# The 32 batches of a layer kernel written out without a loop, with every wait on a constant

## The reference, cut to what matters

```python
# attention: 16 heads of 16, causal and linear
q, k, v = relu(q), relu(k), v            # from xn @ wqkv
kv  = cumsum(k[..., :, None] * v[..., None, :], axis=tokens)
num = einsum('bhnd,bhnde->bhne', q, kv)
den = einsum('bhnd,bhnd->bhn', q, cumsum(k, axis=tokens)) + EPS
attention = (num / den) @ wo
# ffn: sigmoid router, top 2 of 8 experts, 4 of them are MLPs
hid = silu(xn @ Wg) * (xn @ Wu);  mlp_out = hid @ Wd
ffn = sum of cw * (mlp_out, xn, xn, relu(xn)) + causal depthwise conv(xn, 4 taps)
```

## Time and profile before

| | us |
|---|---|
| median of 3 runs | 1405.55 (1403.64 to 1406.98) |
| the profiled execution, its own time | 1406.35 |
| span of its trace | 1404.5 |
| PE busy | 1366.1 (97%) |
| DVE busy | 1134.5 (81%) |
| POOL busy | 793.2 (56%) |
| ACT busy | 747.5 (53%) |

### The profile page before, as it was taken

One profiled execution on the slowest core, in us unless ns is written; L12 is line 12 of the kernel. 1 busy time (PEld: TensorE's weight loads), 2 busy tenths in 40 slices (PEclk: granted clock), 3 DMA queues, 4 the chain that ended last, 5 costly groups with the idle time before them and its releaser, 6 DMA issues.

```text
span 1404.5 us, 40364 instructions
## 1 busy us (share of the span) xinstructions
PE 1366.1 (97%) x16256; PEld 1140.7 (81%) x16256; DVE 1134.5 (81%) x2692; ACT 747.5 (53%) x1545; POOL 793.2 (56%) x679
## 2 busy tenths in 40 slices
PE   4999999999999999999999999999999999999998
PEld 3788887888888888888888888888887888888886
DVE  5788878888788887878878888788888878888876
ACT  5555555555554555555556545555545555455552
POOL 1655555655466655657555566555565556665554
PEclk9999999999999999999999999999999999999999
DMA  5011101111110111011111111110111111111110
GB/s 161 12 62 62 62 32 33 62 62 62 47 47 32 62 62 63 32 36 58 62 62 47 47 32 62 63 62 32 43 51 63 62 47 46 32 62 46 47 47 17
DMA packets 46729, 72.89 MB, mean 52 GB/s; under 512 B 6481, under 2 KB 42193, under 8 KB 42449
## 3 DMA queue, kind: packets, MB, share of 16 engines
q1 hardware_dynamic: 46544, 70.24, 14.3%
HBM read 53.18 MB, written 17.04 MB: 50 GB/s over the span
## 4 chain that ended last, share of the span: by engine, by line
PE 90%; DVE 5%; issue 3%; ACT 1%; SPq 1%; DMA 0%; POOL 0%; DVEq 0%; ACTq 0%; POOLq 0%
PE gate L294 24%; PE up L294 18%; PE scores L294 14%; PE scores L356 9%; PE num L402 7%; PE num L294 7%; PE num L386 4%; DVE sm L724 2%; PE gate L306 2%; PE scores L338 2%; PE state_sum L392 1%; PE gate L419 1%; DVE cT L735 1%; DVE hid L743 1%; PE num L419 0%
## 5 line engine op out<-in xcount | busy, mean ns | idle before, releaser
L724 DVE TENSOR_TENSOR sm<-scores,tables_s 128x512 f32<-128x512 f32 x512 | 316.6, 679 | 31.9 <-PE scores L356 31.9
L592 POOL TENSOR_TENSOR sg<-sg,cwb 128x512 f32<-128x512 f32 x128 | 187.2, 1463 | 209.9 <-ACT sg L512 209.9
L580 POOL TENSOR_TENSOR x_t<-x_t,same 128x1024 f32<-128x1024 f32 x32 | 80.5, 2517 | 328.7 <-ACT same L496 328.7
L512 ACT ACTIVATE sg<-gate 128x512 f32<-128x512 f32 x128 | 76.7, 599 | 276.6 <-PE gate L294 276.6
L456 ACT ACTIVATE hh<-hid 128x512 fp32r<-128x512 f32 x128 | 80.9, 632 | 243.0 <-DVE hid L743 243.0
L735 DVE SCALAR_TENSOR_TENSOR cT<-xT,conv_ws,cT 128x512 f32<-128x512 f32 x192 | 188.9, 1023 | 0.0
L596 POOL TENSOR_TENSOR hl<-hid,hh 128x512 fp32r<-128x512 f32 x128 | 185.9, 1452 | 0.8 <-ACT hh L456 0.8
L356 PE MATMUL scores<-qp,kT 32*128 32x256 f32 x2048 | 147.2, 401 | 13.5 <-issue 8.8
L743 DVE TENSOR_TENSOR hid<-up,sg 128x512 f32<-128x512 f32 x128 | 87.8, 686 | 86.7 <-POOL sg L592 86.7
L356 PEld LDWEIGHTS scores<-qp,kT 32*128 32x128 f32 x2048 | 93.0, 184 | 56.8 <-issue 36.0
L402 PE MATMUL num<-sm,vp 128*32 128x128 f32 x4096 | 136.6, 274 | 0.0
(11 more groups left out here) (161 smaller groups left out, 3858.0 us busy)
## 6 DMA issues: line engine op xcount, KB each, us to landing
cwb<-cw_rows SPq DMA_DIRECT2D x32, 1024.0 KB, 4.7
x_t<-in_L_attn_x_dram SPq DMA_DIRECT2D x32, 512.0 KB, 3.6
out_dram<-x_t SPq DMA_DIRECT2D x32, 512.0 KB, 3.6
cw_rows<-cwt SPq DMA_DIRECT2D x128, 2.0 KB, 1.4
sm<-in_L_attn_wqkv_dram SPq DMA_DIRECT2D x2, 384.0 KB, 5.3
sm<-in_L_ffn_Wg_dram SPq DMA_DIRECT2D x2, 256.0 KB, 4.6
sm<-in_L_ffn_Wu_dram SPq DMA_DIRECT2D x2, 256.0 KB, 5.8
cwb<-in_L_ffn_Wd_dram SPq DMA_DIRECT2D x1, 512.0 KB, 4.8
```

Of the source, the lines that this page charges most:

```text
L512: act.activation(sg[:, :], GB[:, :], ACT.Silu).then_inc(s_sg, 1)
L580: pool.tensor_tensor(xb, xb, same[:, :, :], ALU.add).then_inc(s_base1, 1)
L592: pool.tensor_tensor(sg[:, :], sg[:, :], cwb[:, e, :], ALU.mult).then_inc(s_sgw, 1)
L724: dve.tensor_tensor(heads.rearrange("p g (a n) -> p g a n", a=2), SB[f][:, :].rearrange("p (g a n) -> p g a n", g=C, a=2), causal_s[:, :]. ...
```

## The change

`rounds` becomes a Python loop over all eight sequences, so that the 32 batches are written out one after the other on every engine, and `s` is a number everywhere. The last argument of `body` (how many batches are still to come, cut at 4) is the same for every batch as before. `settled` and its one call are taken out.

```diff
-        def rounds(engine, body):
-
-            with engine.Fori(0, n_seq - 1) as s:
+        def rounds(body):
+
+            for s in range(n_seq):
                 for j in range(BPS):
-                    body(s, j, BPS)
-            for j in range(BPS):
-                body(n_seq - 1, j, BPS - 1 - j)
+                    body(s, j, min(BPS, (n_seq - s) * BPS - 1 - j))
...
-        def settled(engine):
-
-            engine.wait_ge(set_up, 3)
...
-            rounds(pe, batch)
+            rounds(batch)
...
             def normalise(s, j, k):
                 pool.wait_ge(s_stats, at(s, j, 1, k + 1))
                 pool.tensor_tensor(rstd[:, :], vare[:, :], half[:, :], ALU.pow).then_inc(s_rstd, 1)
-                settled(pool)
                 pool.wait_ge(s_rstd, at(s, j, 1, k + 1))
```

More of the change, by code:

```diff
@@ L283, in _ @@
             spread_cw(0, 0, 0)
-            rounds(sp, batch)
+            rounds(batch)
         @block.tensor
@@ L551, in _ @@
             heads(0, 0, 0)
-            rounds(act, batch)
+            rounds(batch)
         @block.gpsimd
@@ L630, in _ @@
             base(0, 0, 0)
-            rounds(pool, batch)
+            rounds(batch)
         @block.vector
@@ L805, in _ @@
             assert count["setup"] == OWN_SETUP, count
-            rounds(dve, batch)
+            rounds(batch)
 _INS = ["L0_attn_x", "L0_attn_wqkv", "L0_attn_wo", "L0_ffn_Wr", "L0_ffn_router_bias", "L0_ffn_Wg", "L0_ffn_Wu",
```

## The result

The changed kernel takes 1395.76 us in the median (1394.29 to 1398.88), beside 1405.86 us (1403.64 to 1409.79) for the kernel before. The ratio is 0.993, with a 95% interval of 0.9911 to 0.9948: 0.7% less, where 0.6% (1396.8 us) was forecast. The profiled execution took 1397.11 us, with a span of 1395.3 us (forecast: 1395.7).

A forecast was written before the change was run, and what follows sets the result against it. PE, busy for 1366.1 of 1404.5 us, was taken as the bound. PE's turns, 8.80 us, and 0 us for every other term, taken from the median of 1405.55 us, gave 1396.8 us, range 1393.8 to 1401.2.

The forecast's parts named there:

- The turn on PE: At six loop turns PE idles before the next batch's first scores; writing the loop out saves 8.80 us.
- The steps of the sum: Savings on PE: 1.51 us in sequence 0, 7.41 in sequences 1 to 5, 0.12 lost in sequence 6, 0 in 7.
- The cause: PE's taken branch back waits for its target's fetch, 3.3 us against 83 ns untaken; rival, branch isn't the wait, chance 0.06.
- DVE is second in line: Without PE's branch alone, DVE's loop would hold the mask until 212.7 us; with both gone, nothing more counted.
- The waits on constants: Constant waits remove register work from every sequencer, counted 0 us; rival that they give more, 1394.1 us, chance 0.03.
- 42.54 against 42.54: Batch length in us with register waits in the loop and with constants in straight code, taken to bound the register work's price.
- POOL's 0.06 us: POOL's first weighing in a sequence's first batch starts 0.06 us later in straight code; counted 0, at most 1.6 us lost.
- the 42.47 of the straight sequence: Length in us of the first batch of the eighth sequence, already straight code, used as base for every sequence's first batch.
- `settled`: One wait fewer on POOL before xn, for memsets done long ago and off the chain: 0 us.
- the entry: Start of batch 0, held by DVE's transposes and mask, with the loop's register set-up beside it: 0 us.
- the fetched code: Longer code, at most the same 140 packets on PE's queue, 0 us; rivals of late fetches, chances 0.07 and 0.04.
- The size: The whole saving, 8.8 us or 0.6%, with PE's pause at each of six turns about 1.5 us.

The follow-up runs named there:

- the same branch, announced: Kernel before with its loop kept and one instruction added at the top of the body naming the branch back as likely taken: 1396.7 us, ratio 0.9916.
- PE alone straight: Kernel before with only PE written out straight with constant waits, the other engines keeping loop and register waits: 1407.7 us, ratio 0.9982.
- two sequences in the body: Kernel before with two sequences in a loop body that runs three times and two written out behind it, so two turns: 1400.06 us, ratio 0.9924.
- the second chip: Chip of the second group of experiments, where the unchanged kernel before was profiled again: 1409.97 us, span 1408.1 us.
- the third chip: Chip of the last three experiments, where the changed kernel was timed again unchanged: 1395.42 us, ratio 0.989 to the kernel before.
- DVE alone straight: Kernel before with only DVE written out straight, the other engines keeping loop and register waits: 1408.11 us, measured once.
- the one jump over less than a block: One of seven forward jumps on PE, added to the changed kernel at the starts of sequences, each over less than 256 instructions: 1397.26 us, ratio 0.9911.

## Why the prediction was right, point by point

- *The turn on PE, 8.80 us.* Right in place and size. From the first scores of batch 4 to those of batch 28 the changed kernel saves 7.33 us. The steps of the sum for the same stretch, 7.41 - 0.12, are 7.29. The last batch of the first sequence lasts 209.12 - 166.59 = 42.53 us in place of 44.05, 1.52 us (forecast: 1.51). Together 8.85. The rest of the 9.2 us between the spans lies in the start: the first scores of the first batch came 0.47 us earlier (34.19 against 34.66), and that batch took 0.07 longer (47.31 against 47.24). The start differs from execution to execution by more. The medians differ by 10.1 us, more than the profiles; what the last us is isn't shown.
- *The cause.* Shown: the same branch, announced, takes 0.35 us, and the time is that of the straight kernel within the scatter. And the branches that aren't announced end 1.36 to 1.54 us behind the end of a packet of PE's code, whether they last 3.3 us or 3.9.
- *DVE is second in line.* Shown by PE alone straight: the mask 3.50 us behind the scores, and a pause of 1.90 us before the second scores. I had worked out that the mask could not start before 212.7, which is 3.2 us behind scores at 209.52. Of the six, two were at 3.5 and four at 3.16 to 3.24.
- *The waits on constants, 0 us.* The step as I put it was wrong in sign at j = 0. I took 42.54 against 42.54 as proof for all batches, but I had no batch at j = 0 with register waits and no turn before it, and said of POOL's 0.06 us that it doesn't reach the end. It does: with registers such a batch lasts 42.32 to 42.35 us, with constants 42.47, the 0.06 on POOL and as much again on PE. The sum didn't suffer, since it used the 42.47 of the straight sequence as its base. So the turns of the profile before cost about 0.8 us more than the 8.8 (0.13 in each of the six batches behind a turn), and the constants take that much back.
- *`settled`, 0 us; the entry, 0 us; the fetched code, 0 us.* Right. With the wait put back xn moves by 0.07 us and no batch changes; batch 0 takes 47.31 us in place of 47.24; the queue carries 128 packets in place of 140; no new pause appears in any sequence, at whatever place the packets begin.
- *The size.* The price of a turn was taken as fixed, 1.5 us. It is not: 2.1 us with two sequences in the body, 2.0 to 2.2 on the second chip, and with the clock's fall 3.2 and 3.4. On the third chip the same change is worth 15.1 us (1410.54 to 1395.42), a ratio of 0.989 (0.9875 to 0.9905), below the result's interval of 0.9911 to 0.9948. The six turns of the second chip's profile come to nearly as much: from batch 3 to batch 28 it has 1077.83 - 1063.04 = 14.8 us more than the changed kernel. So the size was right where the kernel before takes 1405.9 us, as it did in the profile that the forecast was read from; nothing in that profile told of the dearer turns elsewhere, and it is in part luck that the result came from a chip where the kernel before takes that long.

## What to carry to other kernels

When a loop turns back, look at the branch on each engine's sequencer and at the first instruction behind it, not at the busy rows: what counts is how long the branch lasts, less how far the sequencer is ahead, and then the same for the engine that is next in line. One engine without its turn gave a fifth of the gain (PE) or nothing that could be told (DVE). If the code has a stretch that is written out already, it is the best measure of what the rest would take, but compare like with like (here the first batch of a sequence), for otherwise two small effects cancel unseen. A loop whose back edge is announced gave the same here, within the scatter, as code written out (1396.7 us), and where two waits stand on one instruction, write the one that comes late first.

## What the runs showed of the hardware that I had not expected

- The price of a turn can be read from the packets of code: about 1.0 us until the packet starts, 0.9 to 1.4 us for its 16 KB, and 1.4 us from its end to the end of the branch, in all 20 taken branches of PE that went back without a hint. A jump forward that met a packet under way ended 1.35 to 1.42 us behind it as well. Where the packet took longer, the turn did.
- A pause of PE in otherwise dense work can be followed by a stretch at the lower clock (0.63 us for a product that takes 0.39), 1.3 to 1.6 us of loss. It was so behind four pauses, of 1.83 and 1.87 us (the kernel before, second chip) and 1.88 and 1.90 us (PE alone straight), and not behind four others, of 1.88 and 1.93 us (DVE alone straight) and 2.02 and 2.03 us (two sequences), nor behind any of 1.77 us or less (all of these behind the first batch). So the length of the pause alone doesn't decide; what does is open. In the timed runs on these chips the mean granted clock is 0.993 to 0.998 for the kernel before and 0.998 to 0.999 for the changed one, so such falls are a part of what the change is worth there. That a loop's times scatter more isn't shown: on the third chip they are 1408.62 to 1412.89 us in nine runs for the kernel before and 1393.68 to 1396.9 in four for the changed one.
- ACT's turn took 0.25 us with a body of one sequence and about 2.5 us with one of two, while POOL's stayed at 0.25. For ACT, then, the length of its own loop decides whether its turn stalls. The Trainium skill, "Runtime: NRT & Kernel Launch", section "Instruction fetch mechanics", has a taken branch wait for a fetch when its target lies outside the pages at hand. These runs agree: PE's turns of 3.3 to 3.9 us end behind a packet of code, and the one jump over less than a block that found no packet under way took 0.30 us.
- A wrong hint at a loop's exit stopped PE for 1.24 us in the middle of its first scores, and the batch was 1.7 us longer. A packet of PE's code moved from 1225.68 to 1226.59 us, and PE went on 1.54 us behind its end, about as behind the other fetches; that it is the code behind the loop which was missing is my reading.
